# Residual rows moved from the output projection to the FFN's last stage, W_o pieces in eight places

## The reference, cut to what matters

```python
xn = layernorm(x)                                     # x: [4, 4096, 2048] f32
out = x + attention(xn, W_q, W_k, W_v, W_o) + ffn(xn, w1, b1, ln_g, ln_b, w2, b2)

# attention, one head of 2048, causal
q, k, v = rope(xn @ W_q), rope(xn @ W_k), xn @ W_v
attn = softmax(where(causal, q @ k.T / sqrt(2048), -inf)) @ v @ W_o

# ffn, inner 8192; bitlinear: activations to 8 bits by row, weights to -1, 0, 1
h = gelu(silu(bitlinear(xn, w1, b1)))
h = layer_norm(h, ln_g, ln_b)
ffn = bitlinear(h, w2, b2)
```

## Time and profile before

| | before |
|---|---|
| median of 3 runs | 4069.36 us |
| profiled execution | 4071.65 us |
| its span, slowest core (core 0) | 4070.1 us |
| spans of the 8 cores | 4034.0 to 4070.1 us |
| TensorE busy (PE) | 3582.5 us, 88% |
| VectorE busy (DVE) | 1719.7 us, 42% |
| ScalarE busy (ACT) | 1644.8 us, 40% |
| GpSimd busy (POOL) | 588.6 us, 14% |
| mean granted TensorE clock | 0.950 |
| DMA | 960.89 MB, mean 236 GB/s |

### The profile page before, as it was taken

How to read it: one execution, slowest core, us unless ns; L and a number is a source line. 1 busy time by engine, 2 the same in 40 slices (tenths; PEclk the granted TensorE clock), 3 DMA queues, 4 the chain that set the end, 5 groups by cost and what they waited for, 6 DMA issues and landing times.

```text
span 4070.1 us, 50207 instructions; the slowest of 8 cores (4034.0 to 4070.1 us)
## 1 busy us (share of the span) xinstructions
PE 3582.5 (88%) x17720; PEld 1682.8 (41%) x17812; DVE 1719.7 (42%) x2335; ACT 1644.8 (40%) x2190; POOL 588.6 (14%) x854
## 2 busy tenths in 40 slices
PE   3999977987767898969668799999999999999999
PEld 2445533443333444434223344444444444444444
DVE  4667614544443000223664345263634526354450
ACT  3455523235443555537221342525335252443520
POOL 0333320012211221000000111010110101111010
PEclk9999988998987999989889899999999999999999
DMA  9999999647756999988987667585766758576564
GB/s 233 297 315 321 299 244 309 217 165 248 221 188 191 318 302 279 264 263 293 254 237 223 196 221 235 180 267 170 248 191 221 237 181 255 172 242 200 179 203 160
DMA packets 286679, 960.89 MB, mean 236 GB/s; under 512 B 32736, under 2 KB 49376, under 8 KB 279264
## 3 DMA queue, kind: packets, MB, share of 16 engines
q1 hardware_dynamic: 175008, 558.64, 41.5%
q0 software_dynamic: 83488, 303.08, 26.9%
q10 hardware_dynamic: 27936, 95.96, 8.2%
HBM read 873.66 MB, written 117.44 MB: 244 GB/s over the span
## 4 chain that ended last, share of the span: by engine, by line
PE 61%; DMA 22%; issue 6%; ACT 5%; DVE 4%; POOL 1%; SPq 1%; DVEq 0%; ACTq 0%; POOLq 0%
PE Y L123 24%; PE F L123 18%; PE KP L123 10%; PE AT L123 8%; DMA TR<-tr_in 6%; DMA w1q_scr<-O 2%; DMA WS<-w_in 2%; DMA W<-w2q_scr 2%; DMA w2q_scr<-O 2%; DMA XR<-x_in 1%; DMA U<-wo_in 1%; PE TQ L126 1%; ACT H L129 1%; DMA xn_scr<-XN 1%; ACT O L133 1%
## 5 line engine op out<-in xcount | busy, mean ns | idle before, releaser
L123 PE MATMUL Y<-W,Q2T 128*128 128x512 fp8e4 x4096 | 893.7, 381 | 18.8 <-DMA W<-w2q_scr 17.1
L123 PE MATMUL F<-W1B,XQF 128*128 128x512 fp8e4 x3584 | 798.7, 384 | 27.4 <-DMA W1B<-w1q_scr 19.9
L123 PE MATMUL KP<-XT,WKQ 128*128 128x512 bf16 x3072 | 684.0, 384 | 49.2 <-DVE RT2a L149 43.5
L123 PEld LDWEIGHTS Y<-W,Q2T 128*128 128x128 bf16 x4096 | 401.4, 98 | 508.0 <-issue 31.7
L123 PEld LDWEIGHTS F<-W1B,XQF 128*128 128x128 bf16 x3584 | 351.8, 99 | 449.0 <-issue 48.9
L123 PEld LDWEIGHTS KP<-XT,WKQ 128*128 128x128 bf16 x3072 | 301.9, 99 | 412.9 <-issue 69.3
L129 ACT ACTIVATE JK<-H 128x1024 bf16<-128x1024 f32 x256 | 270.0, 1055 | 457.7 <-DVE H L152 442.7
L152 DVE SCALAR_TENSOR_TENSOR H<-F,DQ,B 128x512 f32<-128x512 f32 x256 | 191.7, 750 | 546.7 <-PE F L123 546.7
L133 ACT ACTIVATE O<-WS,nmag 128x1024 fp8e4<-128x1024 f32 x256 | 287.0, 1143 | 310.8 <-DVE WS L143 119.3
L129 ACT ACTIVATE WS<-WS 128x1024 f32<-128x1024 f32 x256 | 270.1, 1055 | 267.4 <-DMA WS<-w_in 260.8
L152 DVE SCALAR_TENSOR_TENSOR H<-H,HS,GB 128x1024 f32<-128x1024 f32 x256 | 311.9, 1277 | 79.2 <-DMA GB<-g_in 65.9
(11 more groups left out here) (100 smaller groups left out, 2744.9 us busy)
## 6 DMA issues: line engine op xcount, KB each, us to landing
W<-w2q_scr SPq DMA_DIRECT2D x256, 512.0 KB, 5.2
WS<-w_in POOLq DMA_DIRECT2D x226, 512.0 KB, 8.4
W1B<-w1q_scr SPq DMA_DIRECT2D x224, 512.0 KB, 3.9
WS<-w_in ACTq DMA_DIRECT2D x172, 512.0 KB, 10.1
WS<-w_in SPq DMA_DIRECT2D x114, 512.0 KB, 7.9
TR<-tr_in SPq DMA_DIRECT2D x96, 512.0 KB, 15.1
XA<-x_in SPq DMA_DIRECT2D x32, 1024.0 KB, 19.8
B<-b_in POOLq DMA_DIRECT2D x128, 256.0 KB, 3.9
```

The lines of the kernel that those rows point to most:

```text
L123: return self.put(PE, lambda e: e.matmul(out, lhsT, rhs, start=start, stop=stop), waits, sig)
```

## The change

The residual rows are no longer added in the projection, which has one addition a cell left, and four BS buffers in place of three. They are loaded and added in FFN2: `xcload` on POOL's queue into one buffer XR (named xc), `residual` on VectorE at step 3 (t = 0) and step 5 (t = 1) of each quarter, ahead of the block's last addition. W_o pieces may lie in all places but 6 and 7, and there are two more of those, U8 and U9. WS7 is gone. Two BS buffers lie where XQ1 is, so the XQF loads wait for `o_end`.

```diff
--- before.py
+++ after.py
@@ -247,7 +247,7 @@
         self.org += 3904
         assert self.org + END <= nc.sbuf_usable_end
         self.WS = [self.at(f"WS{i}", 1024, F32, BG + 4 * KB * i) for i in range(4)]
-        self.WS += [self.at(f"WS{4 + i}", 1024, F32, R4 + o * KB) for i, o in enumerate((8, 12, 4, 8))]
+        self.WS += [self.at(f"WS{4 + i}", 1024, F32, R4 + o * KB) for i, o in enumerate((8, 12, 4))]
         self.O8 = [self.at(f"O8_{i}", 2048, FP8, o) for i, o in enumerate((BG + 16 * KB, R4 + 2 * KB))]
         identf = self.at("identf", 128, F32, R4)
         a = self.dma(SP, "i0", identf, self.ident_in)
@@ -551,7 +551,7 @@
         if not self.order:
             return
         kind, e, q = self.order[-1]
-        if kind == "o" and slot > 5:
+        if kind == "o" and slot in (6, 7):
             self.left[slot] = waits
             return
         p = self.order.pop()
@@ -733,9 +733,10 @@
         B1 = [self.at(f"B1_{i}", 512, F32, R4 + (12 + 2 * i) * KB) for i in range(2)]
         BA = [self.at(f"BA{i}", 512, F32, R4 + 16 * KB + 2 * KB * i) for i in range(2)]
         B2 = self.at("B2", 512, F32, R4 + 16 * KB)
-        XR = [self.at(f"XR{i}", 512, F32, o) for i, o in
-              enumerate((R2 + 64 * KB, R4 + 12 * KB, R4 + 14 * KB))]
-        BS = [self.at(f"BS{i}", 512, F32, R2 + (66 + 2 * i) * KB) for i in range(3)]
+        XR = self.at("XR", 512, F32, R4 + 2 * KB)
+        BS = [self.at(f"BS{i}", 512, F32, o * KB) for i, o in
+              enumerate((R2 // KB + 68, R2 // KB + 70, R4 // KB + 8, R4 // KB + 10))]
+        self.U += [self.at("U8", 2048, BF16, R4 + 12 * KB), self.at("U9", 2048, BF16, R2 + 64 * KB)]
         W1A = [self.at(f"W1A{i}", 4096, FP8, o) for i, o in
                enumerate((R2 + 64 * KB, R2 + 68 * KB, R3 + 24 * KB, R3 + 28 * KB))]
         W1B = [self.at(f"W1B{i}", 4096, FP8, BG + 2 * KB + 4 * KB * i) for i in range(4)]
@@ -792,6 +793,7 @@
         h_free, hsq = {}, {}
         gb_ld, gb_free, qb_pe = {}, {}, {}
         q2_pe, q2_ev, d2_t, b_st = {}, {}, {}, {}
+        xc_ld, y0_t = {}, {}
         nf, nq, nyo = [0], [0], [0]
         jk = [None]
         yorder = [(2 * g + z, e) for g in range(8) for e in range(4) for z in range(2)]
@@ -827,6 +829,16 @@
                 ba_ld[n] = self.dma(POOL, f"ba{n % 2}", BA[n % 2],
                                     self.base_scr[i][:, e * 512:(e + 1) * 512], y_st.get(n - 2),
                                     b_st[i, e], *w)
+
+        def xcload(n, *w):
+            if n < 64:
+                i, e = yorder[n]
+                xc_ld[n] = self.dma(POOL, "xc", XR, self.x_in[2 * i][:, e * 512:(e + 1) * 512],
+                                    y0_t.get(n - 1), *w)
+
+        def residual(n):
+            y0_t[n] = self.tt(BA[n % 2], BA[n % 2], XR, ALU.add, ba_ld[n], xc_ld[n])
+            xcload(n + 1)
 
         def ffn1(g, fill):
             grp = (2 * g, 2 * g + 1)
@@ -973,9 +985,11 @@
                                          W2[k % NW2][:, o * 512:(o + 1) * 512], oc == 0, oc == 63,
                                          w2_ld[k], q2_ev[g], yp_free[bk], sig=(o == 7))
                         w2_pe[k] = pe
+                        if rz == 3 + 2 * t:
+                            residual(n)
                         if rz == 7:
                             y_t[n] = self.stt(BA[n % 2], YP[bk], D2[:, i:i + 1], BA[n % 2], ALU.mult,
-                                              ALU.add, pe, ba_ld[n], d2_t[i])
+                                              ALU.add, pe, y0_t[n], d2_t[i])
                             yp_free[bk] = y_t[n]
                             y_st[n] = self.dma(POOL, f"yo{n % 2}",
                                                self.y[i * 128:(i + 1) * 128, e * 512:(e + 1) * 512],
@@ -1004,21 +1018,13 @@
 
 
         f1_end = w1_pe[31]
-        xr_ld, xr_free = {}, {}
         cells = [(e, i) for e in range(4) for i in range(NO)]
-
-        def xrload(n, *w):
-            if n < 64:
-                e, i = cells[n]
-                xr_ld[n] = self.dma(SP, f"xr{n % 3}", XR[n % 3],
-                                    self.x_in[2 * i][:, e * 512:(e + 1) * 512], xr_free.get(n - 3), *w)
-        for n in range(3):
-            xrload(n, f1_end, b1_free[15])
+        for z in (8, 9):
+            self.fetch(z, f1_end, b1_free[15])
         gbload(0, f1_end)
         gbload(1, f1_end)
         self.bg_eng = ACT
-        for b in (6, 7):
-            self.spare.append((b, (f1_end, *gone)))
+        self.spare.append((6, (f1_end, *gone)))
         fill = pass2(0)
         normed = False
         b2_ld = self.dma(SP, "b2", B2, self.b2_in[:, 0:512])
@@ -1032,28 +1038,25 @@
                             self.u_ld[p], av_ev[i // 4], yp_free[bk], sig=(v == 15 or i == 15))
                 if i == 15 and v % 4 == 3:
                     self.fetch(self.u_at[p], t)
-            yp_free[bk] = self.tt(BS[n % 3], YP[bk], XR[n % 3], ALU.add, t, xr_ld[n],
-                                  b_st.get(cells[n - 3][::-1] if n > 2 else None), f1_end)
-            xr_free[n] = yp_free[bk]
-            a = self.tt(BS[n % 3], BS[n % 3], B2, ALU.add, yp_free[bk], b2_ld)
-            b_st[i, e] = self.dma(SP, f"bs{n % 3}", self.base_scr[i][:, e * 512:(e + 1) * 512],
-                                  BS[n % 3], a)
-            xrload(n + 3)
+            yp_free[bk] = a = self.tt(BS[n % 4], YP[bk], B2, ALU.add, t, b2_ld,
+                                      b_st.get(cells[n - 4][::-1] if n > 3 else None), f1_end)
+            b_st[i, e] = self.dma(SP, f"bs{n % 4}", self.base_scr[i][:, e * 512:(e + 1) * 512],
+                                  BS[n % 4], a)
             if i == 15 and e < 3:
                 b2_ld = self.dma(SP, "b2", B2, self.b2_in[:, (e + 1) * 512:(e + 2) * 512], a)
             if n > 3 and n % 2 == 0 and not normed:
                 normed = next(fill) == "normed"
             if n == 48:
-                self.retire = {6, 7}
+                self.retire = {6}
             if n < 58:
                 self.tick(0.8)
         assert normed
-        o_end = [t, a, b_st[13, 3], b_st[14, 3], b_st[15, 3]]
+        o_end = [t, a, *(b_st[i, 3] for i in range(12, 16))]
         for _ in self.bg:
             pass
         assert not self.retire
         for i in (2, 3):
-            xload(i, self.retired[6], self.retired[7])
+            xload(i, self.retired[6], *o_end)
         for k in range(32, 36):
             w1load(k, *self.bg_end)
         for n in (16, 17):
@@ -1064,7 +1067,8 @@
             gbload(n, *o_end)
         for n in range(2):
             baload(n, *o_end, *self.bg_end)
-        self.qb_w = (b_st[13, 3], b_st[14, 3], b_st[15, 3])
+        xcload(0, *self.bg_end)
+        self.qb_w = tuple(o_end)
         next(fill)
         ffn1(1, fill)
         for _ in fill:
```

## The result

The changed kernel takes 4113.5 us where the kernel before takes 4076.9 on the same chip (medians of 8 runs each): ratio 1.0084, 95% interval 1.0061 to 1.0108. It is slower by 0.8%, and 4034 was predicted.

The account below looks back on a forecast made before the run. TensorE and the DMA engines were taken to bound the output projection in turn. 4071.65 − 75 (projection) + 4 (step) + 35 (FFN2) = 4035.7; with the runs' median 2.3 below the profiled run, forecast 4034 us, range 3995 to 4064.

Parts of the forecast that it names:

- the residual in FFN2: XR loads and additions moved into FFN2 cost 5 us a group, 7 groups, plus 35 us (from 4 to 84).
- The path from base 5 to y7: At a group's end in FFN2, POOL's round trips run from 2481.6 to 2512.7, making y7 6.2 us later.
- 8 × 0.69 us cost nothing by themselves: In FFN2, a group's eight new additions are free on VectorE, which idles 9.4 us for a GB load.
- 1.3 us, inside the 5: In FFN2, two XR issues a group on POOL could be lengthened beside VectorE: 1.3 us, within the 5 us a group.
- The projection: Output projection: waits for U and the XR work go, the stage takes 241 us, a gain of 75.
- 301 for full engines: Output projection: full DMA engines move 301 GB/s, from 265 at 88% busy; 44 MB take 146 us.
- The B2 waits: Output projection: the late bias row leaves up to 6 us of waiting at two changes of quarter, inside the 241.
- The step into group 1: Between projection and FFN group 1: XQF and W1B loads go out later, plus 4 us (from 2 to 8).
- The three signs named in advance: No TensorE wait for U in the projection; F waits for H 5 to 8 us; y7 11 us after FFN2's end.
- Four: Rival in FFN2: XR 3 late in every group, 2 us there and about 9 at y7, 4113 in all; chance 0.10.
- Two: Rival: TensorE bounds the projection, stage 222, and POOL's round trips in FFN2 hide; 3992 us; chance 0.20.
- three: Rival in the projection: rounding comes late, VectorE waits for WS, stage 270 instead of 241, 4065 us; chance 0.14.

Follow-up runs that it names:

- the better order: Changed kernel with XR loaded once and the second row tile's residual put behind the first's y: 4021.0 us.
- both waits mended: Changed kernel with two XR buffers and the second row tile's residual behind the first's final addition: ratio 1.000 to the kernel before.
- the two experiments on B2: Changed kernel with W_o pieces asked for behind B2, ratio 1.008 to before; with two B2 buffers and three BS, 1.007.

## Why the prediction was wrong

**The failed step is the residual in FFN2:** 5 us a group were taken and 14.0 measured, with 84 as the upper end where 98 came. It has four parts.

1. *The chain started too early.* The path from base 5 to y7 was worked out fairly well: 31.1 us (2481.6 to 2512.7), and 33.0 measured on core 2 (2435.73 to 2468.7, y7 being the second of the pair that starts at 2467.99), 33.6 on the mean. It was hung on the time at which base 5 goes out in the kernel before. Base 5 itself is issued 4.1 us later (mean -16.4 for -20.5). y3, whose store it waits for, is 3.7 us late: two additions, 1.4, and 2.3 of waiting for XR 3 ahead of residual 3. y7 was forecast 11.75 us behind FFN2's end and is 17.2.
2. *XR 5 took 9.9 us, not 5.9.* It lies behind two GB loads of 0.5 MB. The prediction named "one of the longest (10.0) and medians" as 10 to 12 later and took the median. From issue to use, XR 7 with no GB load ahead takes 4.6 us on the mean, XR 5 behind two of them 9.6, XR 3 behind four 16.0. Loads with company ahead of them in the queue want the long end of their row.
3. *"8 × 0.69 us cost nothing by themselves" and "1.3 us, inside the 5".* The idle 9.4 us of VectorE lie ahead of a GB load, but the work behind that load is unbroken. Where the change puts them the additions alone make y7 3.4 us late and cost 4.0 a group, in part because residual 5 makes y4 wait for base 5; in the better order y7 is 1.7 late, or 0.7 on cores 0 to 3. The transfers alone make it 4.9 late. All of it with both waits mended makes 8.1; the single XR buffer and the order make the other 5.0 of 13.1. The 1.5 to 2.5 us between 8.1 and the parts' sum I can't assign.
4. *The arithmetic stopped short.* The prediction's own path gave y7 6.2 us later, past a slack already used up, and wrote down 5. By the 1.07 found above its own y7, 11.75, would cost 8.2 us a group on the mean; the other 5.8 are base 5's later issue (2.9 us against the forecast's -19.3) and the 2.5 us by which the path is longer.

**The projection: right in kind, 10 us short.** 64 us of 75. The waits for U went; no other wait for the rounding came. The term that was mis-sized is the rate of the transfers: 53.4 MB in 186 us is 287 GB/s, built on 301 for full engines, and with the engines 99% busy the first 156 us moved 264; at that rate the same sum gives 257. (That no window of some 20 us reaches 358 GB/s, as the prediction has it, holds for the projection, 304 at most; earlier in the kernel before, 690 to 710 moved 359 and 750 to 770 moved 368.) The B2 waits were "up to 6 us at two changes", and are 14 and 15. The fault is where they were counted from: TensorE's four cells (13.8 us at 3.46 a cell) run from the quarter's last matmul, and B2 is asked for only when VectorE has evicted it, 6.2 us later on core 2 (16 cells of 3.46 us from 1938.13 end at 1993.5; issue 1999.70). 21.0 us to its use less the 7.6 then left is 13.4, near the 14.16 of the row. In the two experiments on B2 its wait shrank or went, and the stage gave none of it back.

**The step into group 1:** plus 4 forecast, 0.5 measured with the stage behind it (+2.0 - 1.5), and the first F 14.4 us behind the last cell where 16 was said. The three signs named in advance, no waits for U, F waiting for H, y7 late, all came; H's wait was 13 a group for the 5 to 8 said.

**The rivals.** Four had the right total (4113) by luck: TensorE hardly stopped within FFN2 for a bank (4.2 us in all, on three cores), where it put 2 us a group, and its 9 us at y7 were to come from XR 3 alone. But a small part of its mechanism is there: XR 3 is late behind four GB loads, and though this stays within the 6 us that it called free, the 2.3 us that residual 3 waits pass on to base 5. The main forecast left this out. Two had the group's end free and the stage at 222, where it takes 251; three's late rounding did not come (0.6 us). The Trainium skill's rule on descriptors written beside VectorE's two-port operations (SBUF — State Buffer, the "DVE blocks DMA" trap) is borne out: an issue of 1.03 us, base 5's at 2435.73, stands among those of 0.54, beside VectorE's TENSOR_SCALAR on QB (2435.41, 1.23 us). That is 0.5 us; the loads' cost lay in their bytes and places, not in that.

## What to carry to other kernels

A load taken out of a stage that is short of DMA can lose more than it gave back (here 98 us for 64) if its new place holds a chain of round trips; read the new place's chain (store, wait, load, addition) from the last instruction back, and start the sum from a chain whose first link is already moved by the change. Where several small causes feed one late instruction, measure that instruction's start and not the kernel's time: it ordered ten kernels here to within 0.6 us, where ratios could not. An idle gap on an engine covers new work only if the gap lies behind that work, not ahead of the chain that ends last.

## What the hardware showed beyond the expected

An accumulating DMA from memory to memory worked at next to no cost beside FFN1, where the DMA engines were 68% busy with it and 58% without: FFN1 takes 125.8 us, for 125.5 without any residual. 1 MB from x_in to base_scr took 18.2 us to landing in the burst on core 0 and 12.2 in the later groups, the issue 0.9 us on POOL. The row of the DMA view of core 0, 2150 to 2300:

```profile
base_scr<-x_in POOLq DMA_DIRECT2D x4, 1024.0 KB, 18.2
```

With the DMA engines 97 to 100% busy they moved 273 to 280 GB/s, and 205 in the 15 us of TensorE's first wait (2007 to 2022), on one core of eight that all do the same; the prediction had taken 301 from windows at 88%. These figures count what is written, and a W_o piece is read at twice that size. And a bias row of 0.25 MB took 18.0 us at the median in that stage, against 3.7 us for the same size from POOL over the whole kernel.
